# Two cross-attention layers on one core: norm sums with GpSimd adds and a column tile per head

## What is computed

```python
scores_t = jnp.einsum('bhsd,bhtd->bhst', q, k_t) * attn_scale
probs_t = jax.nn.softmax(scores_t, axis=-1)
text_out = jnp.einsum('bhst,bhtd->bhsd', probs_t, v_t)
attn_scores = jnp.einsum('bhsd,bhnd->bhsn', q, k_ip) * attn_scale
qsem = _l2norm(jnp.einsum('bhst,bte->bhse', probs_t, text_ehs))
sem = jnp.einsum('bhse,bne->bhsn', qsem, _l2norm(ip_ehs))
probs_ip = jax.nn.softmax(attn_scores + 0.5 * sem, axis=-1) * spatial_mask[None, None, :, None]
out = (text_out + probs_ip @ v_ip) @ W_out + b_out + residual
```

## Time and profile before

| | us |
|---|---|
| median of 3 runs | 2812.94 (2812.1 to 2813.39) |
| the profiled execution | 2810.17 |
| its span in the profile | 2808.4 |
| mean granted TensorE clock | 0.988 |

### The profile page before, as it was taken

How to read it: one execution, slowest core, us unless ns; L and a number is a source line. 1 busy time by engine, 2 the same in 40 slices (tenths; PEclk the granted TensorE clock), 3 DMA queues, 4 the chain that set the end, 5 groups by cost and what they waited for, 6 DMA issues and landing times.

```text
span 2808.4 us, 61414 instructions
## 1 busy us (share of the span) xinstructions
PE 2666.7 (95%) x25096; PEld 2083.7 (74%) x25096; DVE 1709.4 (61%) x3464; ACT 1253.6 (45%) x2265; POOL 468.7 (17%) x681
## 2 busy tenths in 40 slices
PE   6899999999999999999999999999999999999977
PEld 5677777777777777777777777777777777777755
DVE  3465666765666755666755666655666655667654
ACT  2344444444444444444444444444444444444443
POOL 1111121111121111121111111111111111111100
PEclk8999999999999999999999999999999999999988
DMA  7576546665546765546764556674557665567630
GB/s 196 97 85 87 83 80 83 90 85 84 84 78 84 93 85 81 82 76 90 88 90 79 83 77 86 83 98 76 82 80 88 84 91 80 83 83 85 85 35 7
DMA packets 450078, 236.31 MB, mean 84 GB/s; under 512 B 220459, under 2 KB 449787, under 8 KB 449788
## 3 DMA queue, kind: packets, MB, share of 16 engines
q1 hardware_dynamic: 433958, 209.34, 55.9%
q10 hardware_dynamic: 15840, 23.04, 2.7%
HBM read 166.38 MB, written 64.59 MB: 82 GB/s over the span
## 4 chain that ended last, share of the span: by engine, by line
PE 76%; DVE 13%; SPq 3%; ACT 3%; DMA 3%; issue 2%; POOL 0%; DVEq 0%; ACTq 0%; POOLq 0%
PE R L715 7%; PE ST L672 6%; PE R L569 5%; PE PN L689 5%; PE PN L745 5%; PE R L559 4%; PE R L616 4%; PE PN L732 4%; DVE m L899 4%; PE R L565 3%; PE R L718 3%; PE R L720 3%; PE R L629 3%; PE R L630 3%; PE R L766 2%
## 5 line engine op out<-in xcount | busy, mean ns | idle before, releaser
L1133 ACT ACTIVATE p<-ST 128x1344 f32<-128x1344 f32 x320 | 413.3, 1291 | 155.3 <-PE ST L675 149.5
L715 PE MATMUL R<-pr,Gh 128*128 128x448 f32 (+1 forms) x960 | 369.9, 385 | 28.4 <-DVE acc L801 28.4
L804 DVE SCALAR_TENSOR_TENSOR w<-p,pr 128x1344 f32<-128x1344 f32 x160 | 249.3, 1558 | 227.0 <-ACT pr L1148 227.0
L801 DVE TENSOR_TENSOR rem<-R,kst 128x375 f32<-128x375 f32 (+1 forms) x160 | 87.6, 547 | 485.2 <-ACT kst L1028 485.2
L801 DVE TENSOR_TENSOR w<-R,w 128x448 f32<-128x448 f32 (+1 forms) x480 | 290.7, 622 | 104.0 <-PE R L720 95.5
L629 PE MATMUL R<-wvh,ch 128*128 128x320 f32 (+3 forms) x896 | 302.8, 338 | 11.2 <-DVE cl L801 10.9
L630 PE MATMUL R<-wvh,cl 128*128 128x320 f32 (+3 forms) x896 | 279.6, 312 | 0.0
L672 PEld LDWEIGHTS ST<-Qs,Ks 100*128 100x128 bf16 (+1 forms) x3520 | 189.1, 98 | 88.0 <-issue 32.9
L1194 POOL TENSOR_TENSOR kst<-rem,kst 128x375 bf16<-128x375 f32 (+1 forms) x160 | 146.6, 916 | 618.7 <-ACT kst L1028 319.9
L672 PE MATMUL ST<-Qs,Ks 100*128 100x112 bf16 (+1 forms) x3520 | 228.7, 214 | 15.5 <-DMA Qs<-ms 6.8
L1148 ACT ACTIVATE pr<-ST 128x1344 fp32r<-128x1344 f32 x160 | 205.3, 1283 | 82.2 <-PE R L720 82.2
(11 more groups left out here) (178 smaller groups left out, 5761.7 us busy)
## 6 DMA issues: line engine op xcount, KB each, us to landing
Ks<-k_split SPq DMA_DIRECT2D x384, 140.6 KB, 6.4
k_split<-kst SPq DMA_DIRECT2D x128, 281.2 KB, 3.1
Ks<-k_split SPq DMA_DIRECT2D x384, 93.8 KB, 9.4
Qs<-q_split SPq DMA_DIRECT2D x384, 70.0 KB, 9.2
cT<-in_ctxT ACTq DMA_DIRECT2D x30, 750.0 KB, 4.7
q_split<-qst SPq DMA_DIRECT2D x128, 84.0 KB, 2.0
k_split<-kst SPq DMA_DIRECT2D x64, 140.6 KB, 2.9
xT<-in_xT SPq DMA_DIRECT2D x32, 192.0 KB, 3.2
```

Source lines behind the costliest of these rows:

```text
L715: e.matmul(r[0:nj, 0:QW], Gh[0:ROWS[u], q:q + nj], pr[0:ROWS[u], QW * u:QW * u + QW], start=u == 0, stop=False)
L801: return e.tensor_tensor(to, x, y, op)
L804: return e.scalar_tensor_tensor(out=to, in0=x, scalar=s, in1=y, op0=op0, op1=op1)
L1133: e.activation(p32[i][:].rearrange("p (u q) -> p u q", u=3), st, ACT.Exp).then_inc(p_whole, 1)
```

## The change

Three token chunks of a group were summed in three matmuls over 448 columns. Now, for groups 0 to 3, a new stage ns_add on GpSimd adds chunks 1 and 2 of w to chunk 0, in place, with two adds of 448 columns. TensorE then runs four matmuls over 112 columns, one per head, each in the column tile of that head, with a selector of 5 columns. It does so one iteration later: ns of group g-2 stands behind pv1 of group g-1. Group 4 has no adds: its ns is twelve matmuls over the three chunks and four heads, in iteration 5, right behind the sum of group 3. The rounding step of VectorE still waits for the sum of two groups back, which now stands in the same iteration. The sums lie in partitions 32h + g of NS, over 112 columns. So nss is 128 x 112 with a tile of its own, one transpose takes the place of four, and the reduction into dsum goes; its bank is released by d. PN is cleared as a whole at the start.

```diff
@@ groups1 @@
+                if g < NG:
+                    o.add("ns_add", b, g - 1, prev)
+                if g > 1:
+                    o.add("ns", b, g - 2, before)
+                if g == 2:
                     o.share("NS", 1, ("ns", b), "ns_read", b + 1)
+                if g == NG:
+                    o.add("ns", b, g - 1, prev)
+            before = prev
...
-        in_bank(("ns_T", b), "ns_sum", o.at("ns_T", b))
+        in_bank(("ns_T", b), "d_bound", b + 1)
...
-        sel = sb("sel_sb", [128, NG, 32])
+        sel = sb("sel_sb", [128, NG, NG])
...
-        nss = w2[0][0:96, 0:QW]
+        nss = sb("nss", [128, S])
@@ tensor @@
-                    for j in range(3):
-                        w.wait_ge(w_times_y, 3 * (NG * b + g) + j + 1)
-                        e.matmul(NS[32 * j:32 * j + 32, 0:QW], sel[0:ROWS[j], g, :],
-                                 w2[n % 2][0:ROWS[j], QW * j:QW * j + QW], start=g == 0, stop=g == NG - 1,
-                                 skip_group_check=True).then_inc(ns_mm, 1)
+                    if g < NG - 1:
+                        w.wait_ge(ns_added, 2 * at("ns_add", b, g, n))
+                    for j in range(1 if g < NG - 1 else 3):
+                        if g == NG - 1:
+                            w.wait_ge(w_times_y, 3 * (NG * b + g) + j + 1)
+                        for h in range(GH):
+                            mm = e.matmul(NS[32 * h:32 * h + NG, 0:S], sel[0:ROWS[j], g, :],
+                                          w2[n % 2][0:ROWS[j], QW * j + S * h:QW * j + S * h + S], start=g == 0 and j == 0,
+                                          stop=g == NG - 1 and j == 2, skip_group_check=True)
+                    mm.then_inc(ns_mm, 1)
...
-                    for h in range(GH - 1):
-                        e.transpose(r[0:S, 96 * h:96 * h + 96], nss[:, S * h:S * h + S], ident[0:96, 0:96])
-                    e.transpose(r[0:S, 288:384], nss[:, 336:448], ident[0:96, 0:96]).then_inc(ns_T, 1)
+                    e.transpose(r[0:S, 0:128], nss[:], ident[:]).then_inc(ns_T, 1)
@@ vector @@
-                    e.memset(PV, 0.0)
+                    e.memset(PN[:], 0.0)
...
                     if k > 2:
-                        w.wait_ge(ns_mm, 3 * (k - 2))
-                    if k > NG:
-                        w.wait_ge(ns_T, (k - 1) // NG)
+                        w.wait_ge(ns_mm, k - 2)
...
-                    parts_sum(by_g, R[slot["R", ("ns_T", b)]][0:S, 0:384].rearrange(
-                        "p (h j g) -> p g h j", j=3, g=32)[:, 0:NG]).then_inc(ns_sum, 1)
-                    w.wait_ge(ns_sum, b + 1)
                     w.wait_ge(dve_step, own.n)
                     stt(d2[:].rearrange("p (g h) -> p g h", h=GH), zq[:].rearrange("p (g h) -> p g h", h=GH), EPS2 / 2,
-                        by_g, ALU.mult, ALU.max).then_inc(d_bound, 1)
+                        R[slot["R", ("ns_T", b)]][0:S, 0:128].rearrange("p (h g) -> p g h", g=32)[:, 0:NG], ALU.mult,
+                        ALU.max).then_inc(d_bound, 1)
@@ scalar @@
-                    w.wait_ge(ns_mm, 3 * NG * (b + 1))
+                    w.wait_ge(ns_mm, NG * (b + 1))
...
-                    copy(nss, NS[0:96, 0:QW]).then_inc(ns_read, 1)
+                    copy(nss[:], NS[:, 0:S]).then_inc(ns_read, 1)
@@ gpsimd @@
+                elif kind == "ns_add":
+                    b, g, n = key
+                    i = at("ns_add", *key)
+                    for j in range(1, 3):
+                        w.wait_ge(w_times_y, 3 * (NG * b + g) + j + 1)
+                        if j == 2:
+                            w.wait_ge(ns_added, 2 * i - 1)
+                        first = w2[n % 2][0:ROWS[j], 0:QW]
+                        e.tensor_tensor(first, first, w2[n % 2][0:ROWS[j], QW * j:QW * j + QW], ALU.add).then_inc(ns_added, 1)
```

More of the change, by code:

```diff
@@ L170, in groups1 @@
     def groups1(b, between):
-        prev = None
+        prev = before = None
         for g in range(NG + 1):
@@ L186, in groups1 @@
                 o.share("PV", 1, ("pv", prev), "pv_read", prev + 1)
-                o.add("ns", b, g - 1, prev)
-                if g == 1:
+                if g < NG:
[3 more added lines that the diff above has]
+                if g == 2:
                     o.share("NS", 1, ("ns", b), "ns_read", b + 1)
+                if g == NG:
+                    o.add("ns", b, g - 1, prev)
+            before = prev
             between(g, True)
@@ L433, in xattn_two_layers @@
         d2 = sb("d2", [S, H])
-        dsum = sb("dsum", [S, H])
         fus = [sb(f"fus{i}", [S, H, NIP]) for i in range(2)]
@@ L469, in xattn_two_layers @@
         pv_mm, pv_read, pvT, pvT_read, o_added = (sem(n) for n in ("pv_mm", "pv_read", "pvT", "pvT_read", "o_added"))
-        y_mm, w_times_y, ns_mm, ns_read, ns_T, ns_sum = (
-            sem(n) for n in ("y_mm", "w_times_y", "ns_mm", "ns_read", "ns_T", "ns_sum"))
+        y_mm, w_times_y, ns_added, ns_mm, ns_read, ns_T = (
+            sem(n) for n in ("y_mm", "w_times_y", "ns_added", "ns_mm", "ns_read", "ns_T"))
         d_bound, d_root, fused, fus_less, ip_exp, ip_weights, ip_T, ip_T_copied, ip_mm, ip_added, num_read = (
@@ L484, in xattn_two_layers @@
                     "m_hi": m_hi, "w_times_y": w_times_y, "o_T_copied": o_T_copied, "x_added": x_added,
-                    "x1_T_copied": x1_T_copied, "ns_sum": ns_sum, "ip_T_copied": ip_T_copied, "ip_added": ip_added,
+                    "x1_T_copied": x1_T_copied, "d_bound": d_bound, "ip_T_copied": ip_T_copied, "ip_added": ip_added,
                     "kip_rem": kip_rem, "vip_copied": vip_copied, "nip_max": nip_max, "s_max_read": s_max_read,
@@ L804, in stt @@
                 return e.scalar_tensor_tensor(out=to, in0=x, scalar=s, in1=y, op0=op0, op1=op1)
-            def parts_sum(to, x):
-                return e.tensor_reduce(to, x, X, ALU.add)
             for kind, key in o.stages:
@@ L979, in vector @@
                     b, = key
-                    by_g = dsum[:].rearrange("p (g h) -> p g h", h=GH)
                     w.wait_ge(pvT_read, at("pvT", b, 1, 1))
@@ L1414 @@
     kones1[3, TEXT1:KW] = -1e30
-    sel = np.zeros((128, NG, 32), np.float32)
+    sel = np.zeros((128, NG, NG), np.float32)
     for i in range(NG):
```

## The result

| | before | after |
|---|---|---|
| median, us | 2813.16 (2812.1 to 2814.58, 4 runs) | 2763.71 (2761.56 to 2767.64, 4 runs) |
| profiled execution / span | 2810.17 / 2808.4 | 2767.64 / 2765.8 |
| mean granted clock | 0.988 | 0.984 |

The account below looks back on a forecast made before the run. TensorE, busy 95% of the span, was taken as the bound. Per batch 0.76 + 0.65 + 0.20 - 0.17 + 0.24 = 1.68 us; 31 x 1.68 + 1 = 53 us less, so 2760 us, range 2738 to 2785.

Parts of the forecast that it names:

- Iteration 1: Layer 1 groups: its sum is removed, so the output projection starts earlier; 0.79 us gained, taken as 0.76.
- Iteration 2: Layer 1 groups: a 0.86 us sum becomes 0.20 us, so q starts earlier; gain 0.65 us.
- four such matmuls take a third: Length of the new sum on TensorE: a third of the 0.59 us of pv1's twelve matmuls, 0.20 us.
- Iterations 3 and 4: Layer 1 groups: ScalarE's second exponential binds, so only 0.20 us each can be gained; the rest becomes TensorE idle time.
- Iteration 4's rounding step: VectorE: GpSimd's adds start first and hold the step from 1459.58 to 1460.27, making the transposes 0.24 us later.
- rival B: Iteration 4: the rounding step goes before the second add, 0.27 gained where 0.17 was lost; 2746 us, chance 0.25.
- Iteration 5: Layer 1 groups: one 0.86 us sum becomes 0.20 us for group 3 and 0.59 for group 4; gain 0.07.
- Tail: Behind the sums VectorE binds, so the gain is only the slot of the removed reduction dsum, 0.24 us.
- Rival E: New TensorE idle time lowers the granted clock in a layer 1 group: 1.0 us lost per batch, 2845 us, chance 0.03.
- C: Gains of iterations 1 and 2 half eaten by a bank wait or held rounding steps; 1.0 us per batch, 2781, chance 0.16.
- D: Nothing measurable: TensorE's gain is lost where the next scores wait for their rows from ms; 2812 us, chance 0.03.
- F: Four 112-column matmuls do not run beside each other; 1.2 us lost per batch, 2850 us, chance 0.03.

Follow-up runs that it names:

- delay_only: Kernel before with its norm sums one iteration later, still three matmuls of 448 columns, no adds, four transposes: 2805.98 us, ratio 0.9967.
- tiles_only: Kernel before with each sum as twelve column-tiled matmuls, one transpose, no dsum; no delay, no adds: 2811.83 us, ratio 0.9993.
- no_adds: Kernel after without GpSimd's adds: twelve matmuls for every group, still one iteration later: 2786.86 us, ratio 0.99.
- combined: Kernel after plus vbd_early, three weight buffers, no group 2 adds, group 0 summed an iteration later, group 3's second add behind the rounding step: 2744.87 us.
- adds_0_3: Kernel after with GpSimd's adds for groups 0 and 3 only, twelve matmuls for the other groups: 2772.04 us, ratio 0.9851.
- dsum_kept: Kernel after with the reduction into dsum put back, behind the wait for zq: 2770.59 us, ratio 0.9851.
- dsum_beside: Kernel after with the reduction into dsum put back, ahead of the wait for zq: 2765.91 us, ratio 0.9821.
- vbd_early: Kernel after with the DMA into vbd issued in iteration 1 and GpSimd's product on it run ahead of the maxima: 2754.65 us, ratio 0.9782.
- tiles_shift: tiles_only with its first norm sum made 17 times over: 2831.6 us, ratio 1.0048.
- tiles_half: tiles_only with its first norm sum made 9 times over: 2825.81 us, ratio 1.0047.

## Why the prediction was right, and where its steps were off

The time came out at 2763.7 us for 2760, inside the range, and the gains of iterations 1 to 3 came nearly as they were argued. That it came so close was in part luck, since errors of both signs met: 0.43 us per batch one way, 0.61 the other. By its steps:

- **Iteration 1**, forecast 0.76: 0.70 (1.83 to 1.13), and delay_only has the same 0.70. o_mm starts 0.16 us after pv1's 0.59 us are over (1341.45 + 0.59 to 1342.20), where the forecast had 0.05 behind the copies. Both of its conditions end at nearly the same time (the copies at 1341.56 + 0.50 = 1342.06), so this row doesn't tell which of them costs the more. pv1 is column-tiled and o_mm is not, as in iteration 2.
- **Iteration 2**, 0.65: 0.55. The sum takes 0.30 us, not 0.20. The step that failed is "four such matmuls take a third": pv1's 0.59 us for twelve is followed by another column-tiled product, the sum by a full-width one, and that costs 0.10 more (24 records 0.69 in tiles_only, 0.59 in pv1). That the change of tiling is the reason is argued from this one comparison. It agrees with the Trainium skill, TensorEngine Tiling (Array Packing), section "Key Properties", which says that a change of tiling mode drains TensorE.
- **Iterations 3 and 4**, 0.20 each as long as ScalarE's exponential binds: 0.21 and 0.19 by medians. The wait on pr is 0.48 us each, not 0.65, for the sum is dearer. delay_only has all of it, and 12 matmuls cost there no more than four (no_adds, combined): the adds of groups 1 and 2 bring TensorE nothing. The held rounding step of iteration 3 costs nothing, as forecast.
- **Iteration 4's rounding step**, forecast held, 0.24 lost: not held. This is the step that failed, and rival B's order is what happened. The forecast had the first add of group 3 start 1.45 us ahead of the step and the second 1.18 later, so 0.27 ahead. Measured: 1.23 ahead (1358.42 to 1359.65), and a pair takes 2.42 us of which one is 1.14, so the second comes 1.28 later, 0.05 behind the step. The larger part of this error is in the forecast's own clock. It took the two rounding steps 4.85 us apart, as they are in the rows of the kernel before (1454.73 and 1459.58), though it had itself given iteration 3 a gain of 0.20, which brings the second one forward; in the kernel after they are 4.66 apart (1354.99 and 1359.65). The adds came where it had them, 3.43 us behind the first step for 3.40. So the margin of 0.27 loses 0.19 by the clock, 0.03 by this and 0.10 by the pair's pitch, and ends at -0.05; without the 0.19 or without the 0.10 the order would have been the forecast's. Rival B named this margin, and its chance of 0.25 was too low. The forecast's order was priced 0.44 above the other (0.24 lost for 0.20 gained); adds_0_3, where it happens, shows 0.36.
- **Iteration 5**, forecast a gain of 0.07: a loss of 0.03 (2.14 to 2.17). 32 records take 0.88 us, not 0.79, by the same change of tiling.
- **Tail**, forecast 0.24: 0.07 undisturbed (15.17 to 15.10, fourth lowest of each). The step "the gain is dsum's slot there" failed. d needs zq as well, and dsum lay beside zq: from zq to d it was 0.34 us (median) and is 0.27. The row that the forecast took it from the earlier trace rows was moreover of a batch in which zq itself took 0.41 us beside GpSimd's product. dsum_kept and dsum_beside show it from both sides.
- **Not forecast**: the meetings of GpSimd's product with VectorE's small steps, and the clock behind them. The mean of the maxima rose by 0.08 us (15.44 to 15.52) where the lowest fell by 0.07. Rival E looked for the clock in the layer 1 groups, where the waits of 0.48 us left it at 1.00. It fell in four batches in the maxima, for about 2 us each. That the change made this more frequent is not shown: each kernel has one trace, and kernels without adds have one to four such batches too (delay_only, tiles_only, tiles_shift, tiles_half). That this product is the cause is shown by vbd_early, with the timelines of the four batches.

Summed by means: 0.70 + 0.55 + 0.17 + 0.19 - 0.03 - 0.08 = 1.50 us per batch. Other pieces lost 0.05 of it, above all the one from o_mm to the scores of layer 0 (0.09), whose cause was not looked for. That leaves 1.45, the difference of the mean periods; 31 times that is 45 us. The two profiled executions differ by 42.5 (the one of after lies 3.9 above its median), the medians by 49.4. Against the forecast's 1.68 the order in iteration 4 gave 0.43 more (0.19 gained for 0.24 lost). The later start of o_mm and the dearer change of tiling took 0.26 (iterations 1, 2 and 5), iteration 3 0.03 in some longer batches, and the tail 0.32: 0.17 by dsum, 0.15 by the disturbed batches.

The traces agree with the rule of exclusion that the forecast took from the Trainium skill, SBUF — State Buffer, section "Who interferes with whom". The step and the add that come later are lengthened by the overlap (2.09 for 1.56, and 3.81 for 2.42 for the pair), the earlier never, and in no_adds none is. Two of each five rounding steps are held, as forecast, but those of iterations 1 and 3 and not those of iterations 3 and 4. Rivals C, D and F fall with the table: the gains of iterations 1 and 2 are whole, the time is far from 2812, and, against F, 12 matmuls of 112 columns take 0.69 us and do run beside each other.

## What to carry to other kernels

Where two engines exclude each other, work out the start of each to a tenth of a microsecond, and carry both the hold before it and the gains already booked into that clock: here 0.20 us of booked gain, left out, were most of a margin of 0.27. A hold that cost nothing also moved the next one off the path, worth 0.36 us per batch, some 11 us. Before a step is counted as the gain, look at what its successor waits for besides it. And many tiny matmuls are not free even when their sum of durations is: the medians over the batches hid stops of 4 us, which only a table of all batches showed.

## What was not expected of the hardware

- TensorE stood still for 1 to 4 us in up to three batches of ten where a sum of 24 records (0.69 us) and the Q projection met full DMA engines, and half a packet of instructions ahead of it moved this by five batches. Each stop ended 1.4 to 1.9 us behind a packet of the instruction queue. 64 more such matmuls in one go ended in a stop of 8.14 us (tiles_shift, at 183 us).
- A sum of 24 column-tiled records takes 0.69 us up to a full-width matmul, and pv1's 24 records take 0.59 up to another column-tiled product.
- Two adds of 128x448 and 115x448 on GpSimd take 2.42 us though one alone takes 1.14: the second, which waits for the first one's signal, starts 1.28 us after it.
- Three waits of TensorE of about 0.5 us within 3 us were followed by a granted clock of 0.59; two such waits of 0.48, 4.7 us apart, by none. The same three waits stand before each of the twelve falls in delay_only, tiles_only, tiles_shift and tiles_half.
